# Attention 2 of a fused two-layer kernel: maxima and sums placed by transfers, results kept with features on partitions

## What is computed

```python
Q = (layernorm(x) @ Wq.T).reshape(B, QL, 16, 16)
scores = einsum('bqhd,khd->bhqk', Q, K) / 4
attn = softmax(scores, axis=-1)
out = einsum('bhqk,khd->bqhd', attn, V).reshape(B, QL, 256)
x = x + out @ Wo.T
```

## Time and profile before

| | |
|---|---|
| median of 3 runs | 2215.05 us (2213.71 to 2221.87) |
| the profiled execution, its own time | 2222.04 us |
| its span in the trace | 2220.3 us |
| mean granted TensorE clock | 0.929 of full speed |
| busy: PE, DVE, ACT, POOL | 91%, 70%, 61%, 12% of the span |
| stage of attention 2, first score to last value | about 1326 us (681.7 to 2008) |
| the reduction of a max unit, L1023 | 1024 of them, 1242.7 us |
| exponentials, L1471 | 2048 of them, 1109.7 us |

### The profile page before, as it was taken

One profiled execution on the slowest core, in us unless ns is written; L12 is line 12 of the kernel. 1 busy time (PEld: TensorE's weight loads), 2 busy tenths in 40 slices (PEclk: granted clock), 3 DMA queues, 4 the chain that ended last, 5 costly groups with the idle time before them and its releaser, 6 DMA issues. The chain is left out here.

```text
span 2220.3 us, 40217 instructions
## 1 busy us (share of the span) xinstructions
PE 2023.1 (91%) x16004; PEld 1010.8 (46%) x16004; DVE 1563.3 (70%) x1931; ACT 1358.0 (61%) x2694; POOL 261.5 (12%) x278
## 2 busy tenths in 40 slices
PE   6793999995478999999999999999999999998995
PEld 3552889994223333333333333333333333445773
DVE  2337212214588999999999998999999999322554
ACT  1220444440015888888888887888888888663321
POOL 0000434431310000000000000000000000001373
PEclk9795999996667999999999998999999999988997
DMA  4201667864726000006001106100002000001134
GB/s 141 75 15 62 209 223 257 257 208 143 107 52 72 13 2 14 13 1 70 13 2 14 13 2 70 13 2 13 13 12 70 2 2 1 11 20 36 34 102 164
DMA packets 150843, 141.21 MB, mean 64 GB/s; under 512 B 75610, under 2 KB 123206, under 8 KB 149894
## 3 DMA queue, kind: packets, MB, share of 16 engines
q1 hardware_dynamic: 141254, 112.98, 21.6%
q0 software_dynamic: 9408, 25.70, 3.6%
HBM read 106.40 MB, written 31.72 MB: 62 GB/s over the span
## 5 line engine op out<-in xcount | busy, mean ns | idle before, releaser
L1023 DVE TENSOR_REDUCE maxp<-banks 128x2 f32<-128x1024 f32 x1024 | 1242.7, 1224 | 59.9 <-PE banks L1017 58.9
L1471 ACT ACTIVATE pring<-banks 128x512 f32<-128x512 f32 x2048 | 1109.7, 595 | 205.2 <-PE banks L1346 91.5
L1360 PE MATMUL banks<-pring,vcur 128*17 128x256 f32 x8192 | 654.5, 392 | 9.6 <-ACT osb L1465 4.1
L1346 PE MATMUL banks<-qst,kst 50*128 50x512 f32 x2048 | 519.0, 503 | 1.2 <-DMA qst<-mrow 1.0
L1017 PE MATMUL banks<-kst,qst 48*128 48x512 f32 x2048 | 437.0, 424 | 27.5 <-DVE maxp L1023 24.7
L1346 PEld LDWEIGHTS banks<-qst,kst 50*128 50x128 f32 x2048 | 194.5, 186 | 446.0 <-ACT pring L1471 419.9
L1360 PEld LDWEIGHTS banks<-pring,vcur 128*17 128x17 f32 x8192 | 137.2, 95 | 372.3 <-issue 205.3
L1017 PEld LDWEIGHTS banks<-kst,qst 48*128 48x128 f32 x2048 | 201.0, 193 | 75.0 <-DVE maxp L1023 67.2
L773 ACT ACTIVATE hT<-banks,b 128x128 f32<-128x128 f32 x295 | 108.5, 368 | 188.0 <-PE banks L704 172.9
L911 DVE TENSOR_SCALAR yo<-banks,wblock 128x256 f32<-128x256 f32 x59 | 28.5, 484 | 224.8 <-PE banks L713 224.8
L1326 POOL TENSOR_TENSOR acc<-xn,orec 128x256 f32<-128x256 f32 x15 | 9.3, 621 | 1250.3 <-DVE orec L1516 1250.3
(11 more groups left out here) (298 smaller groups left out, 1338.6 us busy)
## 6 DMA issues: line engine op xcount, KB each, us to landing
w1r<-in_L_ffn_w SPq DMA_DIRECT2D x59, 640.0 KB, 4.4
kst<-key_parts SPq DMA_DIRECT2D x18, 512.0 KB
key_parts<-ksp SPq DMA_DIRECT2D x32, 256.0 KB, 3.4
w2all<-in_L_ffn_w SPq DMA_DIRECT2D x12, 640.0 KB, 7.8
w2all<-expert_rows SPq DMA_DIRECT2D x12, 512.0 KB, 8.7
qst<-query_parts SPq DMA_DIRECT2D x96, 64.0 KB, 2.3
normed_rows<-xn SPq DMA_DIRECT2D x8, 512.0 KB, 2.9
kf<-in_kT SPq DMA_DIRECT2D x16, 256.0 KB
```

Source lines behind the costliest of these rows:

```text
L1023: return nc.vector.tensor_reduce(maxp[:, B % 2, :, hp, qt, kb], ps[:, base:base + 2, :], X, ALU.max)
L1346: nc.tensor.matmul(ps[:, score_bank(n), :], kst[g % 2][rows, j // 2, kt * P:(kt + 1) * P], qst[i][rows, j // 2, :], start=True, stop=True) ...
L1360: mm = nc.tensor.matmul(ps[32 * j:32 * j + VC, 7, cols], vcur[g % 2][:, kt, j, :], pring[:, (G % 2) * HG + j, cols], start=(kt == 0 and ha ...
L1471: nc.scalar.activation(pring[:, n % (2 * HG), :], ps[:, score_bank(n), :], ACT.Exp, scale=float(DH) ** -0.5).then_inc(exp_done, 1)
```

## The change

The maxima's and the sums' ways no longer pass through TensorE and ScalarE. `mneg` is split on VectorE (`max_high`, `max_low`), turned by VectorE's transpose within blocks of 32 (`max_turned`), stored to DRAM and loaded from there into the rows of `qst`, which also undoes the blocks. For the first batch this happens at the end of the stage before. The units "turn_max" and "turn_out" leave the list; `AHEAD` goes from 3 to 6 key tiles. The sums are copied by DMA from partition 32j+16 to the 16 partitions of their head in a tile `bc` of 128 x 512, VectorE takes the reciprocal of that whole tile at kt = 14, POOL multiplies `osb` by it, and four DMAs pack the result into `aT`, which now lies over `acc`. Since the results stay with features on partitions, each front loses its first two units (7 to 5), and so does the front of block 3 in the next stage; only the last batch's result is turned on TensorE, and back again (`turn_back`). `EARLY`, the units ahead of the first score, goes from 5 to 8. The diff, cut; of the renumbering of fronts only the parts with new work are shown:

```diff
+            bc = sb("bc", [P, S], F32, l1)
             orec = sb("orec", [P, TB, HG], F32, l1)
-            maxp = sb("maxp", [P, 2, 2, NP, TB, KEYS // 512], F32, l1)
+            maxp = sb("maxp", [P, 2, NP, TB, KEYS // 512], F32, l1)
             mneg = sb("mneg", [P, HG * TB], F32, l1)
-            mres = sb("mres", [HG * TB, P], F32, l1)
-            mrow = sb("mrow", [HG * TB, QP, P], F32R, l1)
+            mparts = sb("mparts", [P, QP, HG * TB], F32R, l1)
+            mrows = sb("mrows", [P, QP * HG * TB], F32, l1)
+            maxima = nc.dram_tensor("maxima", [P, QP * HG * TB], F32).ap()
...
+            def store_maxima(sp, B):
+                sp.wait_ge(rows_ready, B + 1)
+                sp.dma_start(maxima, mrows[:]).then_inc(rows_out, 16)
+
+            def load_maxima(sp, B):
+                sp.wait_ge(rows_out, 16 * (B + 1))
                 for r in range(2):
                     for s in range(QP):
-                        row = r * HALF + SIDE * DH + s
-                        sp.dma_start(f32(qst[i][row:row + 1]).rearrange("o h s -> o (h s)"),
-                                     f32(mrow[r * NP * TB:(r + 1) * NP * TB, s, :])).then_inc(rows_in, 16)
+                        row, n = r * HALF + SIDE * DH + s, (s * 2 + r) * NP * TB
+                        sp.dma_start(f32(qst[B % NB][row:row + 1]).rearrange("o h (t q j) -> o (h t) q j", t=TB, q=4),
+                                     maxima.rearrange("(q n) j -> n q j", q=4)[n:n + NP * TB]).then_inc(rows_in, 16)
...
+            def max_high(dve, B):
+                dve.wait_ge(max_done, B + 1)
+                nc.vector.tensor_copy(mparts[:, 0, :], mneg[:]).then_inc(high_done, 1)
+
+            def max_low(dve, B):
+                dve.wait_ge(high_done, B + 1)
+                nc.vector.tensor_tensor(mparts[:, 1, :], mneg[:], f32(mparts[:, 0, :]), ALU.subtract).then_inc(low_done, 1)
+
+            def max_turned(dve, B):
+                dve.wait_ge(low_done, B + 1)
+                if B:
+                    dve.wait_ge(rows_out, 16 * B)
+                nc.vector.transpose(mrows[:], f32(mparts[:]).rearrange("p s n -> p (s n)")).then_inc(rows_ready, 1)
...
+                        store_maxima(sp, 0)
+                        load_maxima(sp, 0)
...
+                        max_high(dve, 0)
+                        max_low(dve, 0)
+                        max_turned(dve, 0)
...
-            FRONTS = [[0, 1, 3, 4, 7, 8, 10], [5, 6, 9, 11, 14, 15, 17], [13, 16, 18, 19, 22, 23, 26]]
-            AHEAD = 3
+            aT = acc[:].rearrange("p t d -> p (t d)").rearrange("p (b k s) -> p b k s", b=NB, k=KD)
+
+
+            FRONTS = [[0, 1, 5, 6, 8], [4, 7, 12, 13, 15], [11, 14, 19, 20, 23]]
+            AHEAD = 6
...
-                for B in range(BATCHES - 1):
-                    plan[(B + 1) * NKT - AHEAD].append(("turn_max", B + 1, 0))
-                    plan[(B + 1) * NKT + 2].append(("turn_out", B, 0))
...
-            EARLY = 5
+            EARLY = 8
             plan = schedule()
-            first = [("turn_max", 0, 0)] + [("max", 1, u) for u in range(EARLY)]
-            tail = ("turn_out", BATCHES - 1, 0)
...
+            first = [("max", 1, u) for u in range(EARLY)]
+            tail = [("turn_out", BATCHES - 1, 0), ("turn_back", BATCHES - 1, 0)]
...
+            def spread_sums(sp, B):
+
+                sp.wait_ge(sums_taken, B + 1)
+                for j in range(HG):
+                    sp.dma_start(bc[32 * j:32 * j + DH, :], osb[32 * j + DH:32 * j + DH + 1, :].unsqueeze(1).to_broadcast([1, DH, S])
+                                 ).then_inc(spread_in, 16)
+
+            def pack(sp, B):
+
+                g, i = divmod(B, NB)
+                sp.wait_ge(out_done, B + 1)
+                for j in range(HG):
+                    row = (g % 2) * HG * DH + j * DH
+                    sp.dma_start(aT[row:row + DH, i, g // 2, :], osb[32 * j:32 * j + DH, :]).then_inc(packed, 16)
...
+                        if B:
+                            spread_sums(sp, B - 1)
+                            pack(sp, B - 1)
                         if B + 1 < BATCHES:
-                            sp.wait_ge(rows_ready, B + 2)
-                            load_maxima(sp, (B + 1) % NB)
+                            store_maxima(sp, B + 1)
+                            load_maxima(sp, B + 1)
...
+                        if B == BATCHES - 2:
+                            norm_pool(pool, NB, main)
+                        pool.wait_ge(rec_done, B + 1)
+                        nc.gpsimd.tensor_tensor(osb[:], osb[:], bc[:], ALU.mult).then_inc(out_done, 1)
...
-                            for t in range(TB):
-                                mm = nc.tensor.transpose(ps[:, FB, t * P:(t + 1) * P], acc[:, TB * LB + t, n * P:(n + 1) * P], ident[:])
+                            for t in range(2 * n, 2 * n + 2):
+                                for k in range(KD):
+                                    mm = nc.tensor.matmul(ps[:, FB, (t % 2) * D:(t % 2 + 1) * D], aT[:, LB, k, t * P:(t + 1) * P],
+                                                          wot[:, k, :], start=(k == 0), stop=(k == KD - 1))
...
-                    units = 0
...
-                    take_units(first)
...
+                            if B > 1:
+                                act.wait_ge(packed, 16 * HG * (B - 1))
                             nc.scalar.copy(osb[:], ps[:, 7, :]).then_inc(sums_taken, 1)
...
+                                max_high(dve, i)
...
+                            dst = bc[:].rearrange("p (t q h d) -> p t q h d", t=TB, q=2, h=HG)[:, :, (NG - 1) % 2]
...
+                        else:
+                            rows = slice((NG - 1) % 2 * HG * DH, (NG - 1) % 2 * HG * DH + HG * DH)
+                            nc.vector.tensor_copy(aT[rows, NB - 1, (NG - 1) // 2, :], ps[rows, base, :]).then_inc(unit_taken, 1)
...
-                    def rest_of_maxima(B):
-
-                        dve.wait_ge(unit_act, nth_taken[flat.index(("turn_max", B, 0))])
-                        dve.wait_ge(mrow_act, B + 1)
-                        nc.vector.tensor_tensor(mrow[:, 1, :], mres[:], f32(mrow[:, 0, :]), ALU.subtract).then_inc(rows_ready, 1)
-
-                    def sums_back(B):
-
-                        dve.wait_ge(unit_act, nth_taken[flat.index(("turn_out", B, 0))])
-                        nc.vector.reciprocal(orec[:], turned.rearrange("p (t h c) -> p t h c", t=TB, h=HG)[:, :, :, DH]
-                                             ).then_inc(outs_ready, 1)
+                    def reciprocals(B):
+                        dve.wait_ge(spread_in, 16 * HG * (B + 1))
+                        nc.vector.reciprocal(bc[:], bc[:]).then_inc(rec_done, 1)
...
+                    RECIPROCAL = 14
...
+                        if B and kt == (RECIPROCAL if B < BATCHES - 1 else 5):
+                            reciprocals(B - 1)
                         for e in plan[G]:
                             unit(*e)
-                    unit(*tail)
+                        if B + 1 < BATCHES and kt == NKT - AHEAD:
+                            max_low(dve, B + 1)
+                        if B + 1 < BATCHES and kt == NKT - AHEAD + 1:
+                            max_turned(dve, B + 1)
...
-            F_STEPS = {(0, 0): 0, (0, 1): 1, (1, 0): 2, (1, 1): 3, (3, 0): 4, (3, 1): 5, (4, 0): 6}
-            RANK_STEP = (8, 0)
-            LIST_STEPS = {(10, 0): 0, (11, 0): 1}
+            EXP_STEP = 4
+            F_STEPS = {(0, 0): 0, (0, 1): 1, (2, 0): 2, (2, 1): 3, (3, 0): 4}
+            RANK_STEP = (7, 0)
+            LIST_STEPS = {(9, 0): 0, (10, 0): 1}
```

More of the change, by code:

```diff
@@ L1243, in schedule @@
                 return plan
-            EARLY = 5
+            EARLY = 8
             plan = schedule()
-            first = [("turn_max", 0, 0)] + [("max", 1, u) for u in range(EARLY)]
-            tail = ("turn_out", BATCHES - 1, 0)
[L1249 to L1256, removed]
-                                  "out_done late_in")
+            first = [("max", 1, u) for u in range(EARLY)]
+            tail = [("turn_out", BATCHES - 1, 0), ("turn_back", BATCHES - 1, 0)]
+            stage_in, score_mm, exp_done, value_mm, sums_taken, unit_mm, unit_taken, spread_in, rec_done, out_done, packed, late_in = \
+                l1_sems("stage_in score_mm exp_done value_mm sums_taken unit_mm unit_taken spread_in rec_done out_done packed late_in")
             LAST_SCORE = (BATCHES - 1) * NKT * HG
@@ L1323, in _ @@
                     for B in range(BATCHES - 1):
[L1324 to L1328 removed]
+                        if B == BATCHES - 2:
+                            norm_pool(pool, NB, main)
+                        pool.wait_ge(rec_done, B + 1)
+                        nc.gpsimd.tensor_tensor(osb[:], osb[:], bc[:], ALU.mult).then_inc(out_done, 1)
+                    for b in range(1, NB - 1):
                         norm_pool(pool, NB + b, main)
@@ L1405, in unit @@
                             mm = front_products(pe, i, u, base)
```

(50 more changed lines are left out.)

92 lines of the change are left out of this document (33 added, 59 removed).

## The result

The changed kernel takes 2265.0 us (median of five runs, 2259.6 to 2294.4) against 2215.05 us: **2.2% slower**, ratio 1.0224, interval 1.0198 to 1.0249. The profiled execution is the longest of the five, 2294.36 us with a span of 2292.6; what tells it from the other four is the granted clock, 0.897 against 0.912 to 0.916, and it is read here with that in mind.

The account below looks back on a forecast made before the run. TensorE was taken to set attention 2's pace, VectorE having 0.09 us spare per unit. Terms -25 + 38 + 63 + 7 - 3 - 1 = +79 on 2222.0 us gave 2301, stated as 2302 us; range 2228 to 2328.

Parts of the forecast that it names:

- the first of its cases, the forecast: Attention 2: reciprocal stops TensorE and the clock falls after most stops; 2262 to 2326 us, chance 0.57.
- The pace and the removed turns: Attention 2 batches: TensorE sets 1.222 us per max unit; both turns leaving it saves 1.7 us a batch, -25 us.
- The reciprocal: VectorE at kt = 14: 128 x 512 takes 3.55 us, stops TensorE some 2.75 us in 14 batches, +38 us.
- The clock: TensorE's granted clock halves after 12 of 14 stops; eleven more such stretches at 5.75 us each, +63 us.
- The second case: Rival for attention 2: TensorE's stops stay but the clock doesn't fall, +16, 2238 us; chance 0.20.
- The start: Stage before attention 2 waits for the first batch's maxima transfers, and eight units precede the first score: +7 us (3 to 9).
- The maxima's way, SP's queue, the transpose: Within a batch: DRAM way 6.9 us with 1.7 to spare, thirteen DMAs on SP, small VectorE operations; all hidden, nothing.
- the fourth case: Rival: maxima arrive late through DRAM on top of the predicted stops and falls, +21 us, 2323 up to 2340; chance 0.07.
- Last batch and tail: Turned tiles leave the last fronts, -3 us (-9 to +5); turning back and next stage, -1 us (-3 to +2).
- 12 of 14: Batches 1 to 14 of attention 2: the count of reciprocal stops after which the clock was predicted to fall.

Follow-up runs that it names:

- the runs with 384 and 512 columns: Changed kernel with its reciprocal over 384 of 512 columns, 2282.6 us (ratio 1.021), and with all 512, unmodified, 2290.2 us (1.023).
- the changed kernel's trace of the second chip: The changed kernel itself, unmodified, run again on another chip: 2290.2 us against 2238.9 for the kernel before, ratio 1.023.
- in four pieces: Changed kernel with its reciprocal cut into four of 128 columns at kt = 14, 17, 20 and 23: 2238.2 us against 2237.7 for the kernel before.
- the 128 x 16 layout: Changed kernel with sums inverted as 128 x 16, then spread through DRAM: 2206.4 us with batch 0's maxima transfers moved to the new stage, 2210.8 without.
- the run with 16 columns: Changed kernel with the reciprocal taken over 16 columns in place of 512, all transfers kept: 2210.3 us, ratio 0.990 to the kernel before.
- the filler: Changed kernel with eight constant products of 128 x 256 added on TensorE at kt = 15 of batches 1 to 14: 2276.1 us, ratio 1.014.

## Why the prediction was right, and where its sizes were off

Direction, mechanism and range were right: slower, 2265 in 2228 to 2328. It was the first of its cases, the forecast. By its steps:

- **The pace and the removed turns.** Right. Without the wide reciprocal a batch is 78.6 us, 1.7 below 80.25, as predicted.
- **The reciprocal.** 3.34 us against 3.55, the lower of the two slopes. The Trainium skill's eight repeats (VectorE: DVE Perf Modes, on the fixed hardware budget) would, as an estimate, have made it 4.3; the runs give 6.25 ns a column. The stop is the duration less 0.81 us at three widths, 2.5 us at the full one and 35 us in sum, against 38; 2.23 us of it are one wait, not the 2.75 that were to be seen.
- **The clock.** Right in kind: it fell after 13 of 14 stops in the profiled execution (12 predicted). From first to fifteenth copy the span grew by 65.8 us; with -24 for the turns, +35 for the stops and the 5.9 us of the fall that the kernel before had in batch 8, the falls come to about 61 us, 4.7 each (a little less, since what the late sums of batches 4 and 8 cost is in it); the forecast had twelve at 5.75, 69 us. The price was read from one stretch of 13.6 us, and most are shorter: the usual batch with one is 85.4 us long, 4.3 over 81.1. The second case, with a clock that stays up, is out. The Trainium skill (TensorE: Matmul & The Clock Gate, on HAM oscillation) would have let waits of 2.23 us pass; the runs with 384 and 512 columns speak against it.
- **The start.** +6.2 against +7, and by the wait that was named: the stage's end waits for SP.
- **The maxima's way, SP's queue, the transpose.** Hidden, as said. The transpose took 0.20 us and the store 1.4 to land, less than the 2.3 assumed; no batch waits for its rows, so the fourth case is out. At the key loads the prediction had the spread sums in with 3 us to spare; they came 1.9 and 1.6 us late, and the waits of TensorE in batches 4 and 8 were longer by about that.
- **Last batch and tail.** -3 was predicted with -9 to +5; this is the term whose **range** was too narrow. It is +2.9 in the profiled execution, inside the range, but 86.2 - 105.0 = -19 with the changed kernel's trace of the second chip, whose last batch has a clock of 1.00: the falls in the last batch are worth more than all that was counted there. The tail came to +2.0 - 2.9 = -0.9, against -1.

The sum was 2302 for the profiled execution, and that one took 2294. The median is 37 us under the forecast. Which term was too large for the other four executions is open, since they have no trace; their granted clock (0.912 to 0.916, not 0.897) says that they had fewer or shorter falls. The second chip points at the last batch rather than at the "12 of 14": there the same kernel had a clock of 0.911 with 14 falls of 14, the last batch at full clock, and +51 us. As an estimate, the profiled execution with that last batch would have taken 2294 - (107.9 - 86.2) = 2273 us. The forecast counted falls only behind the reciprocals and took those of the last batch to be the same in every execution. So the direction and the mechanism were earned; that the median, 2265, still lies in the forecast's own 2262 to 2326 has some luck in it, for the same kernel differs by 35 us between executions.

## What to carry to other kernels

Before an operation is widened on an engine, look for two durations of the same operation at small widths: the slope between 4 and 16 columns gave the price at 512 within 6% (3.55 us taken, 3.34 measured), while the nearest wide row, a copy of 0.69 us, was off by a factor of five. Where two engines run in step, find how late the slower-looking one may be (here 0.81 us) and keep each foreign operation on it under that: in four pieces 3.8 us of work cost 0.8 us a batch, in one block 3.3 us cost 2.5 and the clock on top, and in the 128 x 16 layout nothing. And count an idle stretch of TensorE at more than its length: here a stop of 2.5 us mostly took 4.3 more in the clock (85.4 against 81.1 us a batch). Nor is the clock a fixed charge: before a difference of some 20 us between two versions is believed, look whether it is a stretch in which one trace had falls and the other had none.

## What the runs showed of the hardware that was not expected

Between waits of TensorE of 0.63 us and of 1.43 us the falls went from none in twelve batches to eight in twelve, so 0.8 us more idle time changed the outcome of most batches; but a wait of 2.06 us passed once without a fall. Useless products in the place of the idle time kept the clock up in 14 of 14 batches. In the last batch of the run with 16 columns it fell after 11 us in which TensorE was busy 11.00. A power on POOL took 81.9 us for 128 x 512, 0.16 us a column. And fp32 products of 128 x 256 written as one instruction stand in the trace as two (16 records for 8), 0.46 us for both, and the filler had been planned at half of that.
